# One matmul chain for B, C and dt of a selective scan, and the low parts of the B split moved by DMA

## The chip, the cores and the metric

One core of a Trainium2 chip runs the whole program. The metric is the device time of one execution in microseconds (us). Differences within about 0.2% are hard to tell from none for this kernel.

## What is computed

The network is two Mamba layers, a per-channel convolution stage and two attention and MLP layers over four images of 64 by 64 tokens with 96 channels. The change touches the Mamba layers alone. For each layer (channels DIN = 192, states 16, rank 6):

```python
dbl = xc @ xproj_w                      # 38 columns
dt, Bm, Cm = dbl[..., :6], dbl[..., 6:22], dbl[..., 22:]
delta = softplus(dt @ dt_w + dt_b)
dA  = exp(delta[..., None] * A)
dBx = delta[..., None] * Bm[:, :, None, :] * xc[..., None]
h   = scan(h[t] = dA[t] * h[t-1] + dBx[t])     # along the 4096 tokens
y   = (einsum('blds,bls->bld', h, Cm) + Dp * xc) * silu(z)
```

## The kernel before

**Tiles and steps.** `mamba_phase` works in 32 steps. A step is one layer, one pair of images and one chunk of 512 tokens (`ORDER`). The 2 x 192 channels of the pair lie in three groups of 128 partitions: image 0 channels 0 to 127, image 1 the same, and the last 64 channels of both. A step has 48 units, one for each group and state.

**One unit.** PE spreads the B row of the unit over 128 partitions of a PSUM bank (`broadcast_b`, four banks). DVE multiplies the bank by `dx` = delta * xc (`scale_unit`) and scans it with the decay from ACT (`scan_unit`). GpSimd (POOL) multiplies the states by the C row (`unit`), which one DMA has spread over 128 partitions (`load_c`, two states to a load, four loads ahead). PE adds the products up in PSUM (`add_up`).

**Slots.** Every engine has its program written out by hand as slots, one to a unit, and runs it in order. In slot t PE does `broadcast_b(t + 3)`, the epilogue of the step before, `add_up(t - 5)`, then a piece of the prologue of the next step. DVE does `scale_unit(t + 1)`, `scan_unit(t)`, then its extra operations. ACT does `unit(t + 4)` (the decay), a carry copy in every fourth slot, then its extras. A prologue matmul of PE in slot t stands ahead of `broadcast_b(t + 4)`, which DVE needs between its scans of units t + 2 and t + 3: there a long slot of PE shows. An extra of DVE in slot t lies between its scans of units t and t + 1. "Slot 34" below is always the slot in which DVE scans unit 34 of a step.

**The prologue.** Two tables, `EARLY` for the prologues of 30 steps (one of them runs before the first scan) and `LATE` for two, give the slots: layer norm, the projections to x and z (`x01`, `x2`, `z2`, `z01`), two SiLUs on ACT (`silu_x`, `silu_z`, each between two table loads), then the projection to B, C and dt (`proj`), and from dt the softplus chain (`dt`, `v`, `soft`).

**B in three bf16 parts.** B is split in high, middle and low bf16 parts, so that the spreading matmul can be bf16 with 96 rows (3 parts x 2 images x 16 states). `proj` computes B three times, on partitions 0 to 95 (with dt on 96 to 107) of bank 0: six fp32 matmuls, three of 108 columns into bank 0 and three of 32 columns (C) into bank 1. Then the split works in place:

```python
act.activation(dt_rows[rows, :], mm[rows, 0, :], ACT.Copy)          # "hi", L540
act.activation(b_rows[step % 2][:, :], mm[0:DT_AT, 0, :], ACT.Copy)  # "hi", L541, all 96 rows
dve: mm[0:64] -= b_rows[0:64]                                        # "rest", L636
act: b_rows[0:64] = mm[0:64]                                         # "mid",  L548
dve: b_rows[0:32] = mm[0:32] - b_rows[0:32]                          # "low",  L640
```

C is copied to `c32` (L545), stored to DRAM by SP (`store_c`, before the load with number 20 of 24 in a step) and read back spread. SP issues every DMA of this phase, in order.

Of the kernel before, what the change touches and what calls it, by code (L numbers as in the profile page):

```python
# [35 lines left out]
DT_AT = SPLITS * BC_ROWS  # L36
EPS = 1e-5
# [5 lines left out]
for c in range(CHUNKS):  # L43
# [13 lines left out]
    "proj": [30, 31, 32, 33, 34, 35], "hi": [35, 36], "rest": [37], "mid": [38], "low": [39],  # L57
    "dt": [37, 40, 41], "v": [38, 41, 42], "soft": [39, 40, 41, 42, 43, 44],
# [6 lines left out]
    "proj": [29, 29, 30, 30, 31, 31], "hi": [32, 32], "rest": [33], "mid": [34], "low": [35],  # L65
    "dt": [34, 36, 37], "v": [35, 37, 38], "soft": [37, 38, 39, 40, 41, 42],
# [5 lines left out]
SP_AT = 8  # L72
# [16 lines left out]
def bank_uses():  # L89

    table, count = {}, [0, 0]
    for w in range(-1, STEPS + 1):
        norm, rest = [MEAN, VAR], [X_FIRST, G2, Z_FIRST, PROJ, STEP, STEP2]
        out = [OUT] if w >= 1 else []
        if w + 1 >= STEPS:
            stages = out
        elif is_late(w + 1):
            stages = out + norm + rest
        else:
            stages = norm + out + rest  # L100
        for bank in range(2):
            for stage in stages:
                if stage != STEP2 or bank == 1:
                    table[bank, w, stage] = count[bank]
                    count[bank] += 1
    return table
# [23 lines left out]
def mamba_phase(nc, dram, f_dram, x_stats, f_stats):  # L130

    c_dram = nc.dram_tensor("c_map", (2, 2, STATES, CHUNK), FP32, kind="Internal").ap()


    with ExitStack() as ctx:
        def sb(name, shape, dtype=FP32):
# [8 lines left out]
        w_proj = sb("w_proj", [128, 2, GROUPS, DT_AT + 2 * RANK + BC_ROWS])  # L145
        w_dt = sb("w_dt", [DT_AT + 2 * RANK, 2, GROUPS, 128])
# [18 lines left out]
        tmp2 = sb("tmp2", [128, GROUPS, CHUNK])  # L165
# [5 lines left out]
        c32 = sb("c32", [BC_ROWS, CHUNK])  # L171
        dt_rows = sb("dt_rows", [DT_AT + 2 * RANK, CHUNK])
# [21 lines left out]
            (w_proj[:, :, :, :], dram["w_proj"][:, :, :, 0:DT_AT + 2 * RANK + BC_ROWS]),  # L194
            (w_dt[DT_AT:DT_AT + 2 * RANK, :, :, :], dram["w_dt"]),
# [4 lines left out]
        with nc.semaphore("a_exp") as a_exp, nc.semaphore("w_turned") as w_turned, \  # L200
                nc.semaphore("turned_copied") as turned_copied, nc.semaphore("w_folded") as w_folded:
            turned = dt_rows[0:C, 0:2 * 128].rearrange("p (k n) -> p k n", k=2)
# [42 lines left out]
        names = ["x0_loaded", "x1_loaded", "c0_loaded", "c1_loaded", "c2_loaded", "c3_loaded", "c_stored",  # L245
# [8 lines left out]
        (x0_loaded, x1_loaded, c0_loaded, c1_loaded, c2_loaded, c3_loaded, c_stored,  # L254
# [23 lines left out]
        with nc.Block() as block:  # L278
            @block.sync
            def _(sp):  # L280
                def load_x(pair, c):
                    sp.dma_start(x_in[pair][:, :, :],
                                 dram["x"][:, 2 * pair:2 * pair + 2, c * CHUNK:c * CHUNK + CHUNK]).then_inc(x_loaded[pair], 16)

                def load_c(i):

                    k, at = divmod(i, C_LOADS)
                    g, part = divmod(at, C_LOADS // GROUPS)
                    if at == 0:
                        sp.wait_ge(c_stored, 16 * (k + 1))  # L290
                    if i >= C_RING:
                        sp.wait_ge(multiplied, C_STATES * (i - C_RING + 1))
                    for r0, r1, b in (((0, 128, 0),), ((0, 128, 1),), ((0, HALF, 0), (HALF, 128, 1)))[g]:
                        rows = c_dram[k % 2, b, C_STATES * part:C_STATES * part + C_STATES, :].rearrange("s n -> (s n)")
                        sp.dma_start(c_rows[r0:r1, i % C_RING, :, :].rearrange("p s n -> p (s n)"),
                                     rows.unsqueeze(0).to_broadcast([r1 - r0, C_STATES * CHUNK])).then_inc(c_loaded[i % C_RING], 16)

                def store_c(step):

                    sp.wait_ge(bank1_read, USE[1, step - 1, PROJ] + 1)  # L300
                    sp.dma_start(c_dram[step % 2, :, :, :].rearrange("b s n -> (b s) n"), c32[:, :]).then_inc(c_stored, 16)

                def finish(w):

                    layer, pair, c = ORDER[w - 1]
                    for b in range(2):
                        sp.wait_ge(bank_read[b], USE[b, w, OUT] + 1)
                    if layer == 1:
                        sp.dma_start(f_dram[:, 2 * pair:2 * pair + 2, (c + 1) * CHUNK:(c + 2) * CHUNK],
                                     fused[pair][:, :, :]).then_inc(f_stored[pair], 16)  # L310
                    elif c + 1 < CHUNKS:
                        load_x(pair, c + 1)

                load_x(0, 0)
                load_x(1, 0)
                store_c(0)
                for i in range(C_RING):
                    load_c(i)
                for w in range(STEPS):
                    for at in range(C_LOADS):  # L320
                        i = C_LOADS * w + at + C_RING
                        if at == C_LOADS - C_RING and w + 1 < STEPS:
                            store_c(w + 1)
                        if i < STEPS * C_LOADS:
                            load_c(i)
                        if at == SP_AT and w >= 1:
                            finish(w)
                finish(STEPS)
                for pair in range(2):
                    sp.wait_ge(f_stored[pair], 16 * CHUNKS)  # L330

            @block.tensor
            def _(pe):
# [4 lines left out]
                def broadcast_b(n):  # L338
                    k, u = divmod(n, STEP_UNITS)
                    g, s = divmod(u, STATES)  # L340
                    if u == 0:
                        pe.wait_ge(bank0_read, USE[0, k - 1, PROJ] + 1)
# [31 lines left out]
                def prologue(w, at, step):  # L374
# [41 lines left out]
                    for i in due(plan["proj"], at):  # L416
                        g, bank = divmod(i, 2)
                        if g == 0:
                            fill(bank, w, PROJ)
                        pe.wait_ge(xc_ready, step + 1)  # L420
                        rows, off = ((DT_AT + 2 * RANK, 0), (BC_ROWS, DT_AT + 2 * RANK))[bank]
                        last = pe.matmul(mm[0:rows, bank, :], w_proj[:, layer, g, off:off + rows],  # L422
                                         xc[step % 2][:, g, :], start=g == 0, stop=g == GROUPS - 1)
                        if g == GROUPS - 1:
                            last.then_inc(bank_full[bank], 1)
                    for g in due(plan["dt"], at):
# [4 lines left out]
                        rows = slice(DT_AT, DT_AT + 2 * RANK)  # L431
# [15 lines left out]
            def _(act):  # L447
# [27 lines left out]
                def softplus(step, g, stage):  # L475
# [5 lines left out]
                    if stage == 1:  # L481
# [5 lines left out]
                        act.activation(tmp2[:, g, :], zpre[:, g, :], ACT.Ln).then_inc(log_ready, 1)  # L487
                        act.activation(zpre[:, g, :], zpre[:, g, :], ACT.Copy, bias=-1.0).then_inc(um_ready, 1)

                def prologue(w, at, step):  # L490
# [45 lines left out]
                    for i in due(plan["hi"], at):  # L536
                        act.wait_ge(bank_full[i], USE[i, w, PROJ] + 1)
                        if i == 0:
                            rows = slice(DT_AT, DT_AT + 2 * RANK)
                            act.activation(dt_rows[rows, :], mm[rows, 0, :], ACT.Copy).then_inc(dt_copied, 1)  # L540
                            act.activation(b_rows[step % 2][:, :], mm[0:DT_AT, 0, :], ACT.Copy).then_inc(hi_ready, 1)  # L541
                        else:
                            if step > 0:
                                act.wait_ge(c_stored, 16 * step)
                            act.activation(c32[:, :], mm[0:BC_ROWS, 1, :], ACT.Copy).then_inc(bank_read[1], 1)  # L545
                    for i in due(plan["mid"], at):
                        act.wait_ge(rest_ready, step + 1)
                        act.activation(b_rows[step % 2][0:2 * BC_ROWS, :], mm[0:2 * BC_ROWS, 0, :],  # L548
                                       ACT.Copy).then_inc(mid_ready, 1)
# [26 lines left out]
            def _(dve):  # L576
# [49 lines left out]
                def prologue(w, at, step):  # L626
# [6 lines left out]
                    for i in due(plan["rest"], at):  # L633
                        dve.wait_ge(dt_copied, step + 1)
                        dve.wait_ge(hi_ready, step + 1)
                        dve.tensor_tensor(mm[0:2 * BC_ROWS, 0, :], mm[0:2 * BC_ROWS, 0, :],  # L636
                                          b_rows[step % 2][0:2 * BC_ROWS, :], ALU.subtract).then_inc(rest_ready, 1)
                    for i in due(plan["low"], at):
                        dve.wait_ge(mid_ready, step + 1)
                        dve.tensor_tensor(b_rows[step % 2][0:BC_ROWS, :], mm[0:BC_ROWS, 0, :],  # L640
                                          b_rows[step % 2][0:BC_ROWS, :], ALU.subtract).then_inc(bank_read[0], 1)
# [16 lines left out]
            def _(pool):  # L658
# [8 lines left out]
                def softplus(step, g, stage):  # L667
# [6 lines left out]
                    if stage == 3:  # L674
                        pool.wait_ge(lost_ready, nth)
                        pool.tensor_tensor(tmp2[:, g, :], tmp2[:, g, :], tmp1[:, g, :], ALU.subtract).then_inc(log1p_ready, 1)
                    if stage == 4:
                        pool.wait_ge(log1p_ready, nth)
                        pool.tensor_tensor(delta[into][:, g, :], xpre[:, g, :], tmp2[:, g, :], ALU.add).then_inc(delta_ready, 1)
# [869 lines left out]
```

## Time and profile before

| | |
|---|---|
| median of three runs | 4724.49 us (4716.68 to 4725.94) |
| the profiled execution, its own time | 4725.55 us |
| its span | 4723.4 us |
| first scan to last scan (Mamba phase) | 83.31 to about 3132.6 us |
| busy PE, DVE, ACT, POOL over the span | 4159.9, 3580.9, 2405.8, 2469.5 us |

Matmuls are pipelined, so a busy PE is not a PE at its limit. The starts of the scans are the clock of this kernel: a step is the time from one scan of unit 0 to the next.

### The profile page before, as it was taken

The numbers are of one execution on the slowest core, as the hardware profiler recorded it, in microseconds if no ns is written. First come the engines' busy times: TensorE is split into PE (matmuls) and PEld (weight loads), VectorE is DVE, ScalarE is ACT, GpSimd is POOL, SyncE is SP. The second block draws the span as 40 slices with busy tenths as digits, with TensorE's granted clock in tenths as the row PEclk, the third lists the DMA queues.
The fourth block names the chain that finished last, engine by engine and source line by source line (L and its number), as shares of the span: only waits on it lengthen the run. The fifth ranks groups of instructions, "written<-read, shape, count | busy, mean of one in ns | idle before, by whom it ended". The sixth has DMA issues, their size and how long they took to land. (4 is left out here: it accounts for less than half of the span.)

```text
span 4723.4 us, 44868 instructions
## 1 busy us (share of the span) xinstructions
PE 4159.9 (88%) x13922; PEld 1790.8 (38%) x13922; DVE 3580.9 (76%) x4409; ACT 2405.8 (51%) x3937; POOL 2469.5 (52%) x1988
## 2 busy tenths in 40 slices
PE   6999999999999999999999999841989889888964
PEld 2333333333333333333333333311546546555543
DVE  3999999999999999999999999974115415414345
ACT  4666666666666666666766676621013222312223
POOL 3778887888778877887788778740000000000000
PEclk8999999999999999999999999985999999999976
DMA  3444444444444444444444444433010020000000
GB/s 91 141 130 137 136 143 134 135 137 145 135 133 138 142 137 137 136 138 141 136 138 133 144 132 138 126 88 88 21 38 21 6 53 17 17 15 4 17 0 14
DMA packets 135882, 462.03 MB, mean 98 GB/s; under 512 B 20783, under 2 KB 23282, under 8 KB 133822
## 3 DMA queue, kind: packets, MB, share of 16 engines
q1 hardware_dynamic: 135646, 459.18, 32.6%
q8 instruction: 112, 1.84, 0.2%
q14 instruction: 124, 1.02, 0.1%
HBM read 433.64 MB, written 20.97 MB: 96 GB/s over the span
## 5 line engine op out<-in xcount | busy, mean ns | idle before, releaser
L664 POOL TENSOR_TENSOR prod<-states,c_rows 128x512 f32<-128x512 f32 x1536 | 1939.6, 1279 | 589.2 <-DVE states L596 573.6
L596 DVE TENSOR_TENSOR_SCAN states<-decay,carry,bpsum 128x512 f32<-128x512 f32 x1536 | 1937.8, 1262 | 0.0
L353 PE MATMUL ypsum<-prod,identity 128*128 128x512 f32 x3072 | 1582.4, 596 | 0.4 <-POOL prod L664 0.3
L455 ACT ACTIVATE decay<-delta,decay_rate 128x512 f32<-128x512 f32 x1536 | 1078.4, 716 | 722.1 <-DVE states L596 623.4
L583 DVE TENSOR_TENSOR bpsum<-bpsum,dx 128x512 f32<-128x512 f32 x1536 | 1034.9, 674 | 89.8 <-PE bpsum L346 71.7
L346 PE MATMUL bpsum<-b_rows,select 96*128 96x512 bf16 x1536 | 594.2, 387 | 167.6 <-DVE states L596 166.0
L353 PEld LDWEIGHTS ypsum<-prod,identity 128*128 128x128 f32 x3072 | 590.2, 194 | 309.4 <-issue 175.3
L346 PEld LDWEIGHTS bpsum<-b_rows,select 96*128 96x128 bf16 x1536 | 147.7, 96 | 1072.8 <-DVE states L596 669.4
L1063 PE MATMUL convp<-img_hi,w_hi 96*96 96x512 f16 (+1 forms) x1568 | 485.3, 387 | 59.0 <-PEq L1441 43.1
L1411 DVE SCALAR_TENSOR_TENSOR x<-convp,unscale,x_group 96x1024 f32<-96x1024 f32 x16 | 20.4, 1278 | 407.9 <-PE convp L1063 407.9
L1063 PE MATMUL convp<-img_hi,w_lo 128*96 128x512 f16 (+1 forms) x896 | 276.0, 387 | 0.0
L1063 PE MATMUL convp<-img_lo,w_hi 96*96 96x512 f16 x896 | 274.8, 384 | 0.0
L1063 PEld LDWEIGHTS convp<-img_hi,w_hi 96*96 96x96 f16 (+1 forms) x1568 | 193.0, 124 | 200.1 <-issue 64.7
L401 PE MATMUL mm<-h_norm,w_xs 96*64 96x512 f32 x512 | 267.5, 616 | 0.0
L393 PE MATMUL mm<-h_norm,w_xs 96*128 96x512 f32 x512 | 262.9, 599 | 2.7 <-ACT h_norm L509 2.7
L1221 ACT ACTIVATE t_next<-convp 128x768 f32<-128x768 f32 x16 | 12.9, 808 | 438.3 <-PE convp L1074 438.3
L1063 PE MATMUL convp<-img_lo,w_mid 128*96 128x512 f16 x672 | 207.9, 386 | 0.0
L422 PE MATMUL mm<-xc,w_proj 128*32 128x512 f32 (+1 forms) x384 | 199.6, 604 | 0.0
L1083 PE MATMUL tp<-ident,haug 128*96 128x128 f32 (+1 forms) x512 | 84.9, 295 | 99.3 <-DVE haug L1328 98.8
L519 ACT ACTIVATE xpre<-mm,cols 128x512 f32<-128x512 f32 x96 | 65.7, 685 | 200.5 <-PE mm L401 106.2
L1198 ACT ACTIVATE haug<-dev_t 128x3072 f32<-128x3072 f32 x16 | 44.2, 2765 | 207.2 <-DVE dev_t L1321 207.2
L393 PEld LDWEIGHTS mm<-h_norm,w_xs 96*128 96x128 f32 x512 | 98.0, 192 | 128.6 <-issue 123.8
(215 smaller groups left out, 4531.6 us busy)
## 6 DMA issues: line engine op xcount, KB each, us to landing
c_rows<-c_map SPq DMA_DIRECT2D x512, 512.0 KB, 3.7
c_rows<-c_map SPq DMA_DIRECT2D x512, 256.0 KB, 3.9
x_in<-in_x SPq DMA_DIRECT2D x16, 384.0 KB, 6.0
fused_map<-fused SPq DMA_DIRECT2D x16, 384.0 KB, 5.1
work<-fused_map SPq DMA_DIRECT2D x4, 1536.0 KB, 9.6
x<-in_x SPq DMA_DIRECT2D x4, 1536.0 KB, 15.8
x_biased_map<-work SPq DMA_DIRECT2D x4, 1536.0 KB, 7.1
x_group<-x_biased_map SPq DMA_DIRECT2D x16, 384.0 KB, 3.7
```

Of the source, the lines that this page charges most:

```text
L346: pe.matmul(bpsum[:, n % B_BANKS, :], pick, b_rows[k % 2][:, :], start=True, stop=True).then_inc(b_full, 1)
L353: pe.matmul(ypsum[:, group % Y_BANKS, :], identity[:, :], prod[:, n % P_RING, :], start=s == 0, stop=s == STATES - 1).then_inc(summed, 1)
L393: last = pe.matmul(mm[:, b, :], w_xs[:, layer, k, 0:128], h_norm[:, b, k:k + CHUNK], start=k == 0, stop=k == TAPS - 1)
L401: last = pe.matmul(mm[b * HALF:b * HALF + HALF, 0, :], w_xs[:, layer, k, 128:DIN], h_norm[:, b, k:k + CHUNK], start=k == 0, stop=k == TAPS ...
L422: last = pe.matmul(mm[0:rows, bank, :], w_proj[:, layer, g, off:off + rows], xc[step % 2][:, g, :], start=g == 0, stop=g == GROUPS - 1)
L455: act.activation(decay[:, n % RING, :], delta[k % 2][:, g, :], ACT.Exp, scale=decay_rate[:, ORDER[k][0], g, s:s + 1]).then_inc(decay_ready, 1)
L519: act.activation(xpre[:, g, :], mm[:, g % 2, :], ACT.Identity, bias=cols[:, layer, g, at_conv:at_conv + 1]).then_inc(bank_read[g % 2], 1)
L583: dve.tensor_tensor(bpsum[:, n % B_BANKS, :], bpsum[:, n % B_BANKS, :], dx[k % 2][:, g, :], ALU.mult).then_inc(scaled, 1)
L596: dve.tensor_tensor_scan(states[:, n % H_RING, :], decay[:, n % RING, :], bpsum[:, n % B_BANKS, :], carry[:, at, u:u + 1], ALU.mult, ALU.a ...
L664: pool.tensor_tensor(prod[:, n % P_RING, :], states[:, n % H_RING, :], c_rows[:, n // C_STATES % C_RING, n % C_STATES, :], ALU.mult).then_ ...
L1063: last = pe.matmul(convp[0:C, g % 2, half, :], w, img[0:rows, r:r + GROUP_ROWS // 2, kx:kx + SIDE], start=product == 0, stop=i >= CONV_MMS ...
L1083: last = pe.transpose(tp[0:rows, fill % 2, j * TILE:(j + 1) * TILE], haug[:, 4 * c + j, 0:rows], ident[:, :])
```

## The change

B is projected once. The 76 columns (B 32, C 32, dt 12) are one chain of three fp32 matmuls into bank 0. ACT copies dt, then B and C together in fp32 (`bc32`, 64 rows), then the high part of B, all three in one slot. The middle and the low part are computed on partitions 0 to 31 and moved by two small DMAs of SP to partitions 32 to 63 and 64 to 95 of `b_rows` (`move_b`). B and C rows are stored together (`store_rows`), the loads read C from that store. The first `broadcast_b` of a step waits for both moves. The slots of `proj` and of all that follows it are moved: in `EARLY` `hi` from 35 and 36 to 33, `rest` from 37 to 34, `mid` from 38 to 35, `low` from 39 to 36, the dt matmuls and the softplus three slots or so forward. `tmp2` shrinks to one group, with a wait for the group before.

```diff
+C_FROM, DT_ROW = DT_AT + 2 * RANK, 2 * BC_ROWS
...
-    "proj": [30, 31, 32, 33, 34, 35], "hi": [35, 36], "rest": [37], "mid": [38], "low": [39],
-    "dt": [37, 40, 41], "v": [38, 41, 42], "soft": [39, 40, 41, 42, 43, 44],
+    "proj": [30, 31, 32], "hi": [33], "rest": [34], "mid": [35], "low": [36],
+    "dt": [34, 37, 36], "v": [35, 38, 37], "soft": [36, 37, 38, 39, 40, 41],
...
-    "proj": [29, 29, 30, 30, 31, 31], "hi": [32, 32], "rest": [33], "mid": [34], "low": [35],
-    "dt": [34, 36, 37], "v": [35, 37, 38], "soft": [37, 38, 39, 40, 41, 42],
+    "proj": [29, 30, 31], "hi": [32], "rest": [33], "mid": [34], "low": [35],
+    "dt": [33, 36, 35], "v": [34, 37, 36], "soft": [35, 36, 37, 38, 39, 40],
...
-SP_AT = 8
+SP_AT, SP_ROWS_AT, SP_MOVE_AT = 8, 16, 17
...
-                if stage != STEP2 or bank == 1:
+                if bank == (1 if stage == STEP2 else 0 if stage == PROJ else bank):
...
-        tmp2 = sb("tmp2", [128, GROUPS, CHUNK])
+        tmp2 = sb("tmp2", [128, CHUNK])
...
-        c32 = sb("c32", [BC_ROWS, CHUNK])
-        dt_rows = sb("dt_rows", [DT_AT + 2 * RANK, CHUNK])
+        b_mid = sb("b_mid", [BC_ROWS, CHUNK], BF16)
+        b_low = sb("b_low", [BC_ROWS, CHUNK], BF16)
+        bc32 = sb("bc32", [2 * BC_ROWS, CHUNK])
+        dt_rows = sb("dt_rows", [DT_ROW + 2 * RANK, CHUNK])
...
-            (w_proj[:, :, :, :], dram["w_proj"][:, :, :, 0:DT_AT + 2 * RANK + BC_ROWS]),
-            (w_dt[DT_AT:DT_AT + 2 * RANK, :, :, :], dram["w_dt"]),
+            (w_proj[:, :, :, 0:BC_ROWS], dram["w_proj"][:, :, :, 0:BC_ROWS]),
+            (w_proj[:, :, :, BC_ROWS:DT_ROW], dram["w_proj"][:, :, :, C_FROM:C_FROM + BC_ROWS]),
+            (w_proj[:, :, :, DT_ROW:], dram["w_proj"][:, :, :, DT_AT:DT_AT + 2 * RANK]),
+            (w_dt[DT_ROW:DT_ROW + 2 * RANK, :, :, :], dram["w_dt"]),
...
-            turned = dt_rows[0:C, 0:2 * 128].rearrange("p (k n) -> p k n", k=2)
+            turned = decay[0:C, 0, 0:2 * 128].rearrange("p (k n) -> p k n", k=2)
...
+                def broadcast_rows(kind, k, g, first, count, tile, loaded):
+                    for r0, r1, b in (((0, 128, 0),), ((0, 128, 1),), ((0, HALF, 0), (HALF, 128, 1)))[g]:
+                        rows = bc_dram[k % 2, kind, b, first:first + count, :].rearrange("s n -> (s n)")
+                        sp.dma_start(tile[r0:r1], rows.unsqueeze(0).to_broadcast([r1 - r0, count * CHUNK])).then_inc(loaded, 16)
                 def load_c(i):
                     k, at = divmod(i, C_LOADS)
                     g, part = divmod(at, C_LOADS // GROUPS)
                     if at == 0:
-                        sp.wait_ge(c_stored, 16 * (k + 1))
+                        sp.wait_ge(rows_stored, 16 * (k + 1))
                     if i >= C_RING:
                         sp.wait_ge(multiplied, C_STATES * (i - C_RING + 1))
-                    for r0, r1, b in (((0, 128, 0),), ((0, 128, 1),), ((0, HALF, 0), (HALF, 128, 1)))[g]:
-                        rows = c_dram[k % 2, b, C_STATES * part:C_STATES * part + C_STATES, :].rearrange("s n -> (s n)")
-                        sp.dma_start(c_rows[r0:r1, i % C_RING, :, :].rearrange("p s n -> p (s n)"),
-                                     rows.unsqueeze(0).to_broadcast([r1 - r0, C_STATES * CHUNK])).then_inc(c_loaded[i % C_RING], 16)
-
-                def store_c(step):
-
-                    sp.wait_ge(bank1_read, USE[1, step - 1, PROJ] + 1)
-                    sp.dma_start(c_dram[step % 2, :, :, :].rearrange("b s n -> (b s) n"), c32[:, :]).then_inc(c_stored, 16)
+                    broadcast_rows(1, k, g, C_STATES * part, C_STATES,
+                                   c_rows[:, i % C_RING, :, :].rearrange("p s n -> p (s n)"), c_loaded[i % C_RING])
+                def store_rows(step):
+                    sp.wait_ge(rows_ready, step + 1)
+                    sp.dma_start(bc_dram[step % 2, :, :, :, :].rearrange("k b s n -> (k b s) n"), bc32[:, :]).then_inc(rows_stored, 16)
+                def move_b(step):
+                    sp.wait_ge(mid_ready, step + 1)
+                    sp.dma_start(b_rows[step % 2][BC_ROWS:2 * BC_ROWS, :], b_mid[:, :]).then_inc(b_moved, 16)
+                    sp.wait_ge(bank0_read, USE[0, step - 1, PROJ] + 1)
+                    sp.dma_start(b_rows[step % 2][2 * BC_ROWS:, :], b_low[:, :]).then_inc(b_moved, 16)
...
-                store_c(0)
+                store_rows(0)
+                move_b(0)
                 for i in range(C_RING):
                     load_c(i)
                 for w in range(STEPS):
                     for at in range(C_LOADS):
                         i = C_LOADS * w + at + C_RING
-                        if at == C_LOADS - C_RING and w + 1 < STEPS:
-                            store_c(w + 1)
+                        if at == SP_ROWS_AT and w + 1 < STEPS:
+                            store_rows(w + 1)
+                        if at == SP_MOVE_AT and w + 1 < STEPS:
+                            move_b(w + 1)
...
-                        pe.wait_ge(bank0_read, USE[0, k - 1, PROJ] + 1)
+                        pe.wait_ge(hi_ready, k + 1)
+                        pe.wait_ge(b_moved, 32 * (k + 1))
...
-                    for i in due(plan["proj"], at):
-                        g, bank = divmod(i, 2)
+                    for g in due(plan["proj"], at):
                         if g == 0:
-                            fill(bank, w, PROJ)
-                        pe.wait_ge(xc_ready, step + 1)
-                        rows, off = ((DT_AT + 2 * RANK, 0), (BC_ROWS, DT_AT + 2 * RANK))[bank]
-                        last = pe.matmul(mm[0:rows, bank, :], w_proj[:, layer, g, off:off + rows],
+                            fill(0, w, PROJ)
+                            pe.wait_ge(xc_ready, step + 1)
+                        last = pe.matmul(mm[0:DT_ROW + 2 * RANK, 0, :], w_proj[:, layer, g, :],
                                          xc[step % 2][:, g, :], start=g == 0, stop=g == GROUPS - 1)
                         if g == GROUPS - 1:
-                            last.then_inc(bank_full[bank], 1)
+                            last.then_inc(bank0_full, 1)
...
-                        rows = slice(DT_AT, DT_AT + 2 * RANK)
+                        rows = slice(DT_ROW, DT_ROW + 2 * RANK)
...
-                        act.activation(tmp2[:, g, :], zpre[:, g, :], ACT.Ln).then_inc(log_ready, 1)
+                        if nth > 1:
+                            act.wait_ge(delta_ready, nth - 1)
+                        act.activation(tmp2[:, :], zpre[:, g, :], ACT.Ln).then_inc(log_ready, 1)
...
                     for i in due(plan["hi"], at):
-                        act.wait_ge(bank_full[i], USE[i, w, PROJ] + 1)
-                        if i == 0:
-                            rows = slice(DT_AT, DT_AT + 2 * RANK)
-                            act.activation(dt_rows[rows, :], mm[rows, 0, :], ACT.Copy).then_inc(dt_copied, 1)
-                            act.activation(b_rows[step % 2][:, :], mm[0:DT_AT, 0, :], ACT.Copy).then_inc(hi_ready, 1)
-                        else:
-                            if step > 0:
-                                act.wait_ge(c_stored, 16 * step)
-                            act.activation(c32[:, :], mm[0:BC_ROWS, 1, :], ACT.Copy).then_inc(bank_read[1], 1)
+                        act.wait_ge(bank0_full, USE[0, w, PROJ] + 1)
+                        rows = slice(DT_ROW, DT_ROW + 2 * RANK)
+                        act.activation(dt_rows[rows, :], mm[rows, 0, :], ACT.Copy).then_inc(dt_copied, 1)
+                        if step > 0:
+                            act.wait_ge(rows_stored, 16 * step)
+                        act.activation(bc32[:, :], mm[0:2 * BC_ROWS, 0, :], ACT.Copy).then_inc(rows_ready, 1)
+                        act.activation(b_rows[step % 2][0:BC_ROWS, :], mm[0:BC_ROWS, 0, :], ACT.Copy).then_inc(hi_ready, 1)
                     for i in due(plan["mid"], at):
                         act.wait_ge(rest_ready, step + 1)
-                        act.activation(b_rows[step % 2][0:2 * BC_ROWS, :], mm[0:2 * BC_ROWS, 0, :],
-                                       ACT.Copy).then_inc(mid_ready, 1)
+                        if step > 0:
+                            act.wait_ge(b_moved, 32 * step)
+                        act.activation(b_mid[:, :], mm[0:BC_ROWS, 0, :], ACT.Copy).then_inc(mid_ready, 1)
...
-                        dve.wait_ge(dt_copied, step + 1)
                         dve.wait_ge(hi_ready, step + 1)
-                        dve.tensor_tensor(mm[0:2 * BC_ROWS, 0, :], mm[0:2 * BC_ROWS, 0, :],
-                                          b_rows[step % 2][0:2 * BC_ROWS, :], ALU.subtract).then_inc(rest_ready, 1)
+                        dve.tensor_tensor(mm[0:BC_ROWS, 0, :], mm[0:BC_ROWS, 0, :],
+                                          b_rows[step % 2][0:BC_ROWS, :], ALU.subtract).then_inc(rest_ready, 1)
                     for i in due(plan["low"], at):
                         dve.wait_ge(mid_ready, step + 1)
-                        dve.tensor_tensor(b_rows[step % 2][0:BC_ROWS, :], mm[0:BC_ROWS, 0, :],
-                                          b_rows[step % 2][0:BC_ROWS, :], ALU.subtract).then_inc(bank_read[0], 1)
+                        if step > 0:
+                            dve.wait_ge(b_moved, 32 * step)
+                        dve.tensor_tensor(b_low[:, :], mm[0:BC_ROWS, 0, :], b_mid[:, :], ALU.subtract).then_inc(bank_read[0], 1)
```

## Rows read from the trace of the kernel before

**Rows 1.** The waits of DVE, 200 to 3000 us: total, times, longest.

```profile
DVE bpsum L583 <- PE bpsum L346: 65.3, 191, 2.0
```

**Rows 2.** Busy time by engine: one stretch, and the whole step of four stretches.

```profile
1098.14:1119.90 21.76, 21.76 (x55) 7.71 (x53) 20.90 (x25) 18.37 (x32) 13.29 (x11) 1.00 0.47 121
...
sum 94.87, PE 90.13 PEld 31.22 DVE 93.35 ACT 63.30 POOL 77.17; mean PE 22.53 PEld 7.81 DVE 23.34 ACT 15.83 POOL 19.29
```

**Rows 3.** Timeline of PE: start us, duration, line, shapes, count.

```profile
1100.99 0.38 PE L346 MATMUL bpsum<-b_rows,select 96*128 96x512 bf16 x1
...
1102.07 1.02 PE L422 MATMUL mm<-xc,w_proj 128*108 128x512 f32 x2
1102.93 0.38 PE L346 MATMUL bpsum<-b_rows,select 96*128 96x512 bf16 x1
...
1104.10 1.05 PE L422 MATMUL mm<-xc,w_proj 128*32 128x512 f32 x2
1105.08 0.39 PE L346 MATMUL bpsum<-b_rows,select 96*128 96x512 bf16 x1
```

**Rows 4.** Timeline of DVE in the same step.

```profile
1102.02 1.27 DVE L596 TENSOR_TENSOR_SCAN states<-decay,carry,bpsum 128x512 f32<-128x512 f32 x1
...
1112.14 1.27 DVE L596 TENSOR_TENSOR_SCAN states<-decay,carry,bpsum 128x512 f32<-128x512 f32 x1
1113.33 0.67 DVE L636 TENSOR_TENSOR mm<-mm,b_rows 64x512 f32<-64x512 f32 x1
...
1114.51 1.26 DVE L596 TENSOR_TENSOR_SCAN states<-decay,carry,bpsum 128x512 f32<-128x512 f32 x1
...
1116.94 1.26 DVE L596 TENSOR_TENSOR_SCAN states<-decay,carry,bpsum 128x512 f32<-128x512 f32 x1
...
1118.71 0.67 DVE L640 TENSOR_TENSOR b_rows<-mm,b_rows 32x512 bf16<-32x512 f32 x1
...
1119.90 1.26 DVE L596 TENSOR_TENSOR_SCAN states<-decay,carry,bpsum 128x512 f32<-128x512 f32 x1
...
1121.67 1.26 DVE L596 TENSOR_TENSOR_SCAN states<-decay,carry,bpsum 128x512 f32<-128x512 f32 x1
```

**Rows 5.** Timeline of ACT in the same step.

```profile
1106.52 0.72 ACT L455 ACTIVATE decay<-delta,decay_rate 128x512 f32<-128x512 f32 x1
...
1107.24 1.93 ACT L455 ACTIVATE decay<-delta,decay_rate 128x512 f32<-128x512 f32 x3
1111.32 0.59 ACT L540 ACTIVATE dt_rows<-mm 12x512 f32<-12x512 f32 x1 [2.14 <-PE mm L422]
1111.93 0.59 ACT L541 ACTIVATE b_rows<-mm 96x512 bf16<-96x512 f32 x1
1112.43 0.71 ACT L455 ACTIVATE decay<-delta,decay_rate 128x512 f32<-128x512 f32 x1
```

**Rows 6.** Timeline of ACT where the late plan runs.

```profile
3014.91 0.19 ACT L463 ACTIVATE carry<-states 128x4 f32<-128x4 f32 x1
3015.86 0.59 ACT L540 ACTIVATE dt_rows<-mm 12x512 f32<-12x512 f32 x1 [0.75 <-PE mm L422]
3016.47 0.59 ACT L541 ACTIVATE b_rows<-mm 96x512 bf16<-96x512 f32 x1
```

**Rows 7.** Timeline of DVE at that place.

```profile
3017.17 0.69 DVE L636 TENSOR_TENSOR mm<-mm,b_rows 64x512 f32<-64x512 f32 x1 [1.15 <-ACT b_rows L541]
```

**Rows 8.** DMA issues: count, KB each, us to landing.

```profile
c_rows<-c_map SPq DMA_DIRECT2D x512, 512.0 KB, 3.7
...
c_map<-c SPq DMA_DIRECT2D x32, 64.0 KB, 3.8
```

**Rows 9.** Timeline of ACT in the opening, before the first scan.

```profile
66.82 1.28 ACT L535 ACT_TABLE_LOAD   x1
70.06 0.59 ACT L540 ACTIVATE dt_rows<-mm 12x512 f32<-12x512 f32 x1 [1.96 <-PE mm L422]
...
73.01 0.69 ACT L554 ACTIVATE tmp<-mm,cols 128x512 f32<-128x512 f32 x1 [0.32 <-PE mm L432]
```

More of the change, by code:

```diff
@@ L130, in mamba_phase @@
 def mamba_phase(nc, dram, f_dram, x_stats, f_stats):
-    c_dram = nc.dram_tensor("c_map", (2, 2, STATES, CHUNK), FP32, kind="Internal").ap()
+    bc_dram = nc.dram_tensor("bc_map", (2, 2, 2, STATES, CHUNK), FP32, kind="Internal").ap()
     with ExitStack() as ctx:
@@ L144, in mamba_phase @@
         w_z = sb("w_z", [C, 2, DIN])
-        w_proj = sb("w_proj", [128, 2, GROUPS, DT_AT + 2 * RANK + BC_ROWS])
-        w_dt = sb("w_dt", [DT_AT + 2 * RANK, 2, GROUPS, 128])
+        w_proj = sb("w_proj", [128, 2, GROUPS, DT_ROW + 2 * RANK])
+        w_dt = sb("w_dt", [DT_ROW + 2 * RANK, 2, GROUPS, 128])
         w_out = sb("w_out", [128, 2, 2, C])
@@ L243, in mamba_phase @@
             nc.all_engine_barrier(sem_only=True)
-        names = ["x0_loaded", "x1_loaded", "c0_loaded", "c1_loaded", "c2_loaded", "c3_loaded", "c_stored",
+        names = ["x0_loaded", "x1_loaded", "c0_loaded", "c1_loaded", "c2_loaded", "c3_loaded", "rows_ready", "rows_stored", "b_moved",
                  "b_full", "decay_ready", "scaled", "scanned",
@@ L253, in mamba_phase @@
         sems = [ctx.enter_context(nc.semaphore(n)) for n in names]
-        (x0_loaded, x1_loaded, c0_loaded, c1_loaded, c2_loaded, c3_loaded, c_stored,
+        (x0_loaded, x1_loaded, c0_loaded, c1_loaded, c2_loaded, c3_loaded, rows_ready, rows_stored, b_moved,
          b_full, decay_ready, scaled, scanned, carry_saved, multiplied,
@@ L675, in softplus @@
                         pool.wait_ge(lost_ready, nth)
-                        pool.tensor_tensor(tmp2[:, g, :], tmp2[:, g, :], tmp1[:, g, :], ALU.subtract).then_inc(log1p_ready, 1)
+                        pool.tensor_tensor(tmp2[:, :], tmp2[:, :], tmp1[:, g, :], ALU.subtract).then_inc(log1p_ready, 1)
                     if stage == 4:
                         pool.wait_ge(log1p_ready, nth)
-                        pool.tensor_tensor(delta[into][:, g, :], xpre[:, g, :], tmp2[:, g, :], ALU.add).then_inc(delta_ready, 1)
+                        pool.tensor_tensor(delta[into][:, g, :], xpre[:, g, :], tmp2[:, :], ALU.add).then_inc(delta_ready, 1)
                     if stage == 5:
```

## The prediction

> **What bounds the kernel now.** I read the waits of DVE first. In 2800 us of the Mamba phase DVE waits 65.3 us for the spreading matmul of B [rows 1] and for next to nothing else. So the step is DVE's own work plus a little of PE. The busy times of one whole step say the same: DVE 93.35 and PE 90.13 of 94.87 us, ACT 63.30 and POOL 77.17 [rows 2]. ACT has a third of its time free, as a mean. The question is what it has at the place that the change moves to.
>
> Then I read the starts of the scans. With nothing extra a unit takes DVE 1.77 us (1121.67 - 1119.90) [rows 4]. A unit with one small DVE operation behind its scan takes 2.37 (1114.51 - 1112.14, with "rest"), one with the skip 2.43 (1116.94 - 1114.51). The unit with gate and low takes 2.96, so with the gate alone some 2.37 (a small operation adds 0.60). These are the DVE-bound slots. In the others of this stretch PE sets the pace. A PE slot with a 108-column projection takes 1.94 us from one spreading matmul to the next, one with the 32-column projection 2.15 [rows 3], both over 1.77.
>
> The stretch to compare is from the scan of unit 32 (1102.02) to that of unit 40 (1119.90): 17.88 us [rows 4]. Ahead of it nothing is moved, and behind it units take 1.77. It is that of the 29 prologues of the early plan that run under scans (the 30th is the opening); I worked it out for this step and take it for all.
>
> **The change: what it gives PE.** Three of the six projection matmuls go. They were in slots 31, 33 and 35. The gaps that the scans then have, by slot: 32 and 33 each 1.94 (PE's slots 30 and 31), 34 with "rest" 2.37, 35 1.77, 36 with "low" 2.37, 37 1.77, 38 with the skip 2.43, 39 with the gate alone 2.37. Sum 16.96, against 17.88: 0.92 us less a step, if nothing new is waited for. A 76-column matmul has no row here. Its PE slot is bounded by 1.94 and 2.15; I take 1.94, as 76 is nearer to 108 than to 32. It will turn out not to matter.
>
> DVE's work is not less: "rest" has 32 rows for 64, and the "low" operation on 32 rows and the "rest" on 64 both take 0.67 [rows 4].
>
> **What it asks of ACT.** This is the step that decides. "rest" moves from slot 37 to 34, and needs the high part of B, which ACT copies in slot 33. Follow ACT in its own order [rows 5]. The SiLU of z with its two table loads fills slot 31, and ACT comes out of it at 1106.52, with the decay of slot 32. The carry copy follows, and at 1107.24 three decays at once, of slots 33, 34 and 35, which ACT was behind with: 0.61 us each (1.93 for three, the last 0.72). In the kernel before ACT then waits 2.14 us for PE, so it is early for `hi`. After the change `hi` stands behind the decay of slot 33 alone:
>
> - the decay of slot 33 at 1107.24, so the dt copy at 1107.85 (PE is done by then: slot 31 at 1102.93, slot 32 at 1104.87, its matmul 1.08 later, 1.02 long: 1106.97; with 2.15 for the slots, 1107.4)
> - the copy of B and C 0.61 later, at 1108.46 (the pace from the dt copy to the next is 0.61 [rows 5])
> - the high part 0.50 later, at 1108.96 (from L541 to the next is 0.50 [rows 5]; the new copies have 64 and 32 rows, but all these copies run along 512 elements, and 12 rows and 96 rows both took 0.59)
> - "rest" 0.70 behind the start of that copy, at 1109.66 (3016.47 to 3017.17 where DVE did wait for it [rows 6, 7]).
>
> DVE is there sooner: scan 33 at 1103.96, scan 34 at 1105.90, "rest" free to start 1.19 later (1112.14 to 1113.33 [rows 4]), at 1107.09. It stands 2.57 us. DVE runs in order, so behind it stand the scale of unit 35 and the scan after it, and for these wait POOL, PE and ACT. PE's gain is inside this wait, and so is the doubt about 76 columns.
>
> From "rest" to the next scan is 1.18 (1113.33 to 1114.51), so scan 35 starts at 1110.84. Then 1.77, 2.37, 1.77, 2.43, 2.37: scan 40 at 1121.55, where it was 1119.90. A step of the early plan gets 1.65 us longer: -0.92 + 2.57. Times 29: **+47.8 us**.
>
> The old order shows the same wait where the late plan has "rest" one slot behind `hi`: DVE stood 1.15 us by the profile's account [rows 7]. There ACT waited 0.75 us for PE [rows 6]; now it goes on at once: dt 0.1 behind the start of the carry copy (3014.91), "rest" 0.61 + 0.50 + 0.70 later, at 3016.82 for 3017.17. Two steps: **-0.7 us** (none to -1.5).
>
> **The opening.** Before the first scan nothing runs beside the chain. ACT waits 1.96 us for the six matmuls [rows 9]. With three, the dt copy starts when the table load is done, at 68.10 for 70.06. The extra copy ahead of the high part gives back 0.5, but the old dt matmul waited for C's copy. I take **-1.8 us** (bounds -1.4 and -1.96). The loads of `w_proj` come as three DMAs of small pieces for one: no row shows that; between -1 (fewer bytes) and +3, taken as 0.
>
> **The moves and the stores, costed at nothing.** `low` starts at about 1113.8 and is done by 1114.5. A transfer from issue to landing takes 3.7 or 3.8 us [rows 8]; the moves are of 32 KB, for 64 KB of the old store. So b_moved is there by 1119. The first spreading matmul of the next step stands in PE's slot 45, behind the scan of unit 44, which ends near 1121.6 + 4 x 1.77 + 1.3 = 1129.9: cover 10 us. If that were gone, each us late is a us a step. SP holds two loads of C while it waits: number 16 until the store is issued (about 1109.1), number 17 until `low` is done (1114.5). They land by 1113.5 and 1119.5, for units 40 and 42, which POOL takes up after 1122.8 and 1126.4: cover 7 us or more. The wait for `tmp2` is on a delta some 20 slots old. `mid` on ACT waits for "rest" (done 1110.4), and the first dt matmul needs only the dt copy, as PE is ahead again. "low" is 2 slots behind "rest", and ACT has the middle part by 1111.4.
>
> **Sum.** 47.8 - 0.7 - 1.8 = +45.3. On the profiled execution's own 4725.55: 4770.9. The median of the runs is 1.06 lower, so 4769.8; I say **4770 us**, 1.0% slower. Bounds: the stall can be 0.4 shorter (dt copy to the next at 0.50, a quicker handover) or 0.5 longer a step, so +34 to +61; with the opening, 4755 to 4789.
>
> **One rule against a row.** The paces of ACT's copies are 0.61 and 0.50 [rows 5]. The Trainium skill, ScalarE: Activation LUTs, Rules for kernel authors, budgets 0.3 us an ACTIVATE and 0.83 ns an element, so an estimate of 0.72 us for 512 elements. By it the stall would be longer, and the whole about 4783; the trace does not agree for the copies that it shows.
>
> **Rivals.**
> 1. *ACT is in time, and PE's gain stands (faster).* For it: ACT idles a third of a step, and waits for PE at this very place before the change. Against it: it is now asked for two decays sooner and has one copy more to make first. It decides at one point: "rest" must start before 1108.01 (1119.90 less the 11.89 from "rest" to scan 40), so the high part before 1107.31, when ACT is still on the decay of slot 33. If there is no stall: 29 x -0.92 = -26.7, the late plans three matmuls of 1.02 us each, so up to -6.1 for both (an estimate: their PE slots hold two of them), -1.8: 4690.9, **4690 us**. 10%.
> 2. *A second wait as well (slower yet).* SP is the suspect: two waits in its queue in front of the loads, and two moves. For it: every DMA of the phase goes by this queue. Against it: covers of 7 and 10 us. If the landing took 1 us more than a cover, +31: **4801 us**. 8%.
> 3. *ACT's copies of 64 rows are longer than those seen*, by some 0.16 each: 29 x 0.47 = +13.6: **4783 us**. 6%. This is what the skill's budget would make of it.
> 4. *ACT comes out of the SiLU earlier once PE is lighter*, so that stall and gain cancel: **4725 us**. 4%. Against it: the table load starts behind z's copies, which the change leaves alone.
>
> Forecast: 72%. Faster by over 0.2% is rival 1 and a quarter of rival 4: 0.11. Within 0.2% (what measurement can tell): 0.03. Slower: 0.86. The range of 8 in 10 is 4742 to 4800; the forecast's own is 4755 to 4789.
>
> **What would show it.** Right: DVE's "rest" waits for ACT's copy of the high part about 2.6 us in each step, some 75 us over the phase; the waits of DVE for the spreading matmul fall; the step shown here 96.5 us long. ACT no longer waits for the projection. Wrong: no wait at "rest", and that step near 94 us; or the wait is at the spreading matmul of unit 0 or in POOL for a load of C.

## The result, and the profile after

| | us |
|---|---|
| before, median of the runs | 4723.89 |
| after, median of 4 runs | 4778.0 (4775.46 to 4779.35) |
| ratio | 1.0117, 95% interval 1.0099 to 1.0134 |
| forecast | 4770 (range 4742 to 4800) |
| profiled execution after, its span | 4777.2 |

The waits of DVE in the same 2800 us, after (total us, times, longest):

```profile
DVE mm L654 <- ACT b_rows L563: 73.5, 29, 3.0
DVE bpsum L602 <- PE bpsum L366: 46.0, 138, 2.0
```

The first row is new. It is 29 waits at "rest" for ACT's copy of the high part: 28 steps of the early plan with 2.52 us each by the profile's account, and one of the two late steps with 2.98 (the first early step and the second late one lie outside these 2800 us, and have the same waits). The wait for the spreading matmul is down from 65.3 [rows 1] to 46.0: the gain is there, and it is small. Here is the stretch from the scan of unit 32 to that of unit 40, on DVE:

```profile
1023.03 1.27 DVE L615 TENSOR_TENSOR_SCAN states<-decay,carry,bpsum 128x512 f32<-128x512 f32 x1
...
1026.90 1.27 DVE L615 TENSOR_TENSOR_SCAN states<-decay,carry,bpsum 128x512 f32<-128x512 f32 x1
1030.69 0.69 DVE L654 TENSOR_TENSOR mm<-mm,b_rows 32x512 f32<-32x512 f32 x1 [2.52 <-ACT b_rows L563]
...
1031.90 1.26 DVE L615 TENSOR_TENSOR_SCAN states<-decay,carry,bpsum 128x512 f32<-128x512 f32 x1
...
1033.67 1.26 DVE L615 TENSOR_TENSOR_SCAN states<-decay,carry,bpsum 128x512 f32<-128x512 f32 x1
1034.85 0.65 DVE L660 TENSOR_TENSOR b_low<-mm,b_mid 32x512 bf16<-32x512 f32 x1
...
1036.03 1.26 DVE L615 TENSOR_TENSOR_SCAN states<-decay,carry,bpsum 128x512 f32<-128x512 f32 x1
...
1042.60 1.26 DVE L615 TENSOR_TENSOR_SCAN states<-decay,carry,bpsum 128x512 f32<-128x512 f32 x1
```

It takes 19.57 us (1042.60 - 1023.03) for 17.88 before [rows 4]; the forecast was 19.53. DVE was free for "rest" at 1028.09 (1026.90 and the 1.19 of [rows 4]) and started it at 1030.69: it stood 2.60 us, for 2.57 forecast. Everything around it goes at the paces forecast: 1.77 and 2.36 behind it. ACT at the same place:

```profile
1027.53 0.72 ACT L473 ACTIVATE decay<-delta,decay_rate 128x512 f32<-128x512 f32 x1
...
1028.26 0.70 ACT L473 ACTIVATE decay<-delta,decay_rate 128x512 f32<-128x512 f32 x1
1028.98 0.59 ACT L559 ACTIVATE dt_rows<-mm 12x512 f32<-12x512 f32 x1
1029.60 0.59 ACT L562 ACTIVATE bc<-mm 64x512 f32<-64x512 f32 x1
1030.09 0.57 ACT L563 ACTIVATE b_rows<-mm 32x512 bf16<-32x512 f32 x1
```

The decay of slot 33 starts at 1028.26, then the dt copy, the copy of B and C and the high part start 0.72, 0.62 and 0.49 us apart, and "rest" 0.60 behind the last. A step like that of [rows 2] went from 94.87 to 96.56 us (+1.69; forecast +1.65). Three early steps are longer still, that of [rows 2] among them; they come under the clock of PE below.

The moves and the store, from issue to landing (count, KB each, us):

```profile
bc_map<-bc SPq DMA_DIRECT2D x32, 128.0 KB, 2.3
...
b_rows<-b_mid SPq DMA_DIRECT2D x32, 32.0 KB, 3.3
b_rows<-b_low SPq DMA_DIRECT2D x32, 32.0 KB, 1.8
```

`low` is done by 1035.5; its move lands some 2 us after its issue, and the first spreading matmul that needs it comes after the scan of unit 44, at about 1051. The cover of 10 us stands. In these 2800 us POOL waits for DVE, PE and ACT, and not once for a load of C.

### The profile page after: what moved, and what is told of

Read it like the earlier page. It is cut to its first block and busy times, and to the rows that moved or that the text cites. A ratio compares the mean times of both kernels' runs of the same rounds, so it can differ in the third digit from the quotient of the medians.

```text
span 4777.2 us, 44613 instructions
## 1 busy us (share of the span) xinstructions
PE 4114.0 (86%) x13730; PEld 1784.4 (37%) x13730; DVE 3575.6 (75%) x4409; ACT 2420.3 (51%) x3937; POOL 2470.5 (52%) x1988
## 3 DMA queue, kind: packets, MB, share of 16 engines
q14 instruction: 126, 1.02, 0.1%
## 5 line engine op out<-in xcount | busy, mean ns | idle before, releaser
L373 PE MATMUL ypsum<-prod,identity 128*128 128x512 f32 x3072 | 1609.7, 606 | 0.4 <-POOL prod L683 0.3
L373 PEld LDWEIGHTS ypsum<-prod,identity 128*128 128x128 f32 x3072 | 599.8, 197 | 305.1 <-issue 170.8
L1102 PE MATMUL tp<-ident,haug 128*96 128x128 f32 (+1 forms) x512 | 84.9, 296 | 99.3 <-DVE haug L1347 98.8
L692 POOL TENSOR_TENSOR tmp<-zpre,tmp 128x512 f32<-128x512 f32 x96 | 122.0, 1270 | 42.5 <-ACT zpre L508 42.5
```

The source lines that it names most:

```text
L373: pe.matmul(ypsum[:, group % Y_BANKS, :], identity[:, :], prod[:, n % P_RING, :], start=s == 0, stop=s == STATES - 1).then_inc(summed, 1)
L692: pool.tensor_tensor(tmp1[:, g, :], zpre[:, g, :], tmp1[:, g, :], ALU.subtract).then_inc(lost_ready, 1)
L1102: last = pe.transpose(tp[0:rows, fill % 2, j * TILE:(j + 1) * TILE], haug[:, 4 * c + j, 0:rows], ident[:, :])
```

## The experiments

All are built from the changed kernel unless it is said otherwise. Times are medians, beside the kernel before on the same chip (4723.19 us for the first four, 4724.76 for the last four).

**rest36: the split two slots later.**

```diff
-"hi": [33], "rest": [34], "mid": [35], "low": [36], "dt": [34, 37, 36], "v": [35, 38, 37],
+"hi": [33], "rest": [36], "mid": [37], "low": [38], "dt": [34, 39, 36], "v": [35, 40, 37],
-SP_MOVE_AT = 17
+SP_MOVE_AT = 18
```

> The changed kernel, with only the split of B two slots later in the early plan (rest 36, mid 37, low 38, the second dt matmul behind it at 39). Theory (DVE stands for ACT's copy of the high part, which is ready 3.76 us after DVE starts the scan of unit 34): DVE reaches rest at 4.73 us after that start, so there is no wait. The stretch from the scan of unit 32 to that of unit 40 is 16.96 us, for 19.6 in the changed kernel and 17.88 in the one before. 29 x 2.57 = 74.5 us less than the changed kernel's 4778: about 4702, faster than before by 0.5%. Rival (the moves, the stores or PE's waits cost the time): still near 4778, with a wait at the spreading matmul of unit 0 or in POOL. Rival (the projection never was a price): 4725.

Measured: 4701.69 us, ratio 0.9954 (0.9937 to 0.9971). DVE in the stretch:

```profile
1004.79 1.27 DVE L615 TENSOR_TENSOR_SCAN states<-decay,carry,bpsum 128x512 f32<-128x512 f32 x1
...
1006.73 1.27 DVE L615 TENSOR_TENSOR_SCAN states<-decay,carry,bpsum 128x512 f32<-128x512 f32 x1
...
1008.50 1.27 DVE L615 TENSOR_TENSOR_SCAN states<-decay,carry,bpsum 128x512 f32<-128x512 f32 x1
1009.69 0.66 DVE L654 TENSOR_TENSOR mm<-mm,b_rows 32x512 f32<-32x512 f32 x1
```

"rest" starts 1.19 us after its scan: no wait. The same matmuls, copies and DMAs, waiting for the same things, are now faster than the kernel before. The stretch takes 17.11 us (1000.92 to 1018.03), where I had said 16.96. With "rest" gone from slot 34, that slot shows PE's 1.94 (1004.79 to 1006.73), which it had hidden.

**rest35: one slot later.** The same edit with 35, 36, 37 and dt at 38.

> The same with the split one slot later (rest 35, mid 36, low 37). Theory: DVE reaches rest 2.96 us after the start of the scan of unit 34 and stands 0.80 us a step; 29 x 1.77 = 51.3 us less than the changed kernel: 4727, the same as before. Rivals: 4778 as for the other.

Measured: 4722.4 us, ratio 1.0 (0.9991 to 1.001). "rest" starts 1.85 us after its scan, for the 1.19 without a wait: it stands 0.66 us in each early step (0.58 by the profile's account), for 0.80 expected. DVE comes to it 0.17 later than expected, as PE's 1.94 in slot 34 comes to light here too; the stretch takes 17.80 us, 1.77 less than in the changed kernel, as expected. Three places of the split give 4778, 4722 and 4702: each slot is worth what DVE does in it, until the wait is used up.

**dt_last: the copies in another order.** The edit in words:

```diff
-act: dt copy, copy of B and C, high part
+act: copy of B and C, high part, dt copy
```

> The changed kernel with ACT's three copies in the order B and C, high part of B, dt. Theory (the price is the queue in front of the high part on ACT, priced by copies): rest starts 0.61 us sooner in every step, the dt matmul 1.1 us later with room. 31 x 0.61 = 18.9 us less: 4759. Rival (DVE waits for something else that ends at the same time): 4778.

Measured: 4751.83 us, ratio 1.0065 (1.0048 to 1.0081). 26 us less, for 19. ACT there:

```profile
1020.04 0.70 ACT L473 ACTIVATE decay<-delta,decay_rate 128x512 f32<-128x512 f32 x1
1020.65 0.57 ACT L561 ACTIVATE bc<-mm 64x512 f32<-64x512 f32 x1
1021.13 0.57 ACT L562 ACTIVATE b_rows<-mm 32x512 bf16<-32x512 f32 x1
```

The first copy of 64 rows starts 0.61 us after the decay (1020.04 to 1020.65), where the dt copy of 12 rows started 0.72 after it, and the next follows in 0.48, where behind the dt copy it took 0.62. So the dt copy held "rest" up by 0.75 us a step (4.25 us for 5.00 from the scan of unit 34 to the next), and 31 x 0.75 is 23. In the profiled executions 24.6 us of the difference lie between the first scan and the last: those 23, and 1.4 because three steps of the changed kernel are 2.8 longer than their like (the clock of PE, below), and here one late and one early step are 1.4 longer together. The order of three small copies is worth nearly half of the loss.

**no_moves: B without its middle and low part.** The two DMAs of `move_b` are left out, the waits for them become waits for `low`, and the rows of `b_rows` for the two parts are zero.

> The changed kernel without the two moves of B: the middle and the low part stay where they are computed, and the rows of b_rows for them are zero, so B counts with its high part alone. The first spreading matmul waits for low directly. Theory (the moves are covered by 10 us): 4778, within 3 us. Rival (SP's queue or the transfers take time from the step): up to 31 us less, near 4747.

Measured: 4778.28 us, ratio 1.012 (1.0103 to 1.0136), the same as the change. The moves have no part in the time. The store of B and C is still there in this run; but POOL waits for no load of C in either kernel, so the rest of rival 2 is out as well.

**silu_z34: the SiLU of z behind the high part on ACT.**

```diff
-"silu_z": [31]
+"silu_z": [34]
```

> The changed kernel with the SiLU of z, and its two table loads, in ACT's slot 34 in place of 31: behind the high part, in front of the middle part. Theory (ACT's order is the price): ACT comes to the high part as soon as PE has the projection, the wait at rest falls from 2.6 to about 1.7 us, and a new wait of about 1.7 us stands at low for the middle part; together 0.8 us a step more: about 4802. Rival (DVE's wait at rest is PE's lateness, not ACT's): the wait at rest stays 2.6.

Measured: 4832.97 us, ratio 1.0233 (1.0217 to 1.0249), 31 us more than expected. ACT and DVE in one step, then PE:

```profile
1045.34 0.59 ACT L559 ACTIVATE dt_rows<-mm 12x512 f32<-12x512 f32 x1 [2.96 <-PE mm L440]
...
1047.05 0.69 DVE L654 TENSOR_TENSOR mm<-mm,b_rows 32x512 f32<-32x512 f32 x1 [1.55 <-ACT b_rows L563]
...
1052.97 0.68 DVE L660 TENSOR_TENSOR b_low<-mm,b_mid 32x512 bf16<-32x512 f32 x1 [1.68 <-ACT b_mid L568]
...
1061.02 0.70 DVE L602 TENSOR_TENSOR bpsum<-bpsum,dx 128x512 f32<-128x512 f32 x1 [0.81 <-PE bpsum L366]
```

```profile
1049.80 1.02 PE L373 MATMUL ypsum<-prod,identity 128*128 128x512 f32 x2
1054.13 2.07 PE L450 MATMUL mm<-dt_rows,w_dt 12*128 12x512 f32 x2 [3.31 <-ACT xpre L574]
...
1056.53 1.92 PE L373 MATMUL ypsum<-prod,identity 128*128 128x512 f32 x2
```

The two waits are those expected, 1.55 and 1.68 us: with the SiLU out of the way ACT itself waits 2.96 us for PE's projection, so what is left of DVE's wait is no longer ACT's backlog, and the block of 4.1 us (two table loads and the SiLU) bites where it stands now. The rest of the loss is new. PE idles 3.31 us behind the stalled chain, and from then its matmuls take twice as long (two passes in 1.92 us for 1.02). So DVE waits again for the spreading matmul, 0.81 us, and the stretch takes 21.27 us. Early steps like this one are 2.07 us longer than in the changed kernel, for 0.8 expected.

**spread: the one chain in every second slot.**

```diff
-"proj": [30, 31, 32], "hi": [33], "rest": [34], "mid": [35], "low": [36],
-"dt": [34, 37, 36], "v": [35, 38, 37], "soft": [36, 37, 38, 39, 40, 41],
+"proj": [31, 33, 35], "hi": [36], "rest": [37], "mid": [38], "low": [39],
+"dt": [37, 40, 41], "v": [38, 41, 42], "soft": [39, 40, 41, 42, 43, 44],
-SP_ROWS_AT, SP_MOVE_AT = 16, 17
+SP_ROWS_AT, SP_MOVE_AT = 18, 19
```

> The one chain in every second slot (proj 31, 33, 35) and all behind it in the slots of the kernel before (hi 36, rest 37, mid 38, low 39, dt and softplus as before). Theory: PE catches up 0.69 us in each empty slot, so the scans of units 32 to 36 go at DVE's 1.77; the stretch from the scan of unit 32 to that of unit 40 is 5 x 1.77 + 2.37 + 2.43 + 2.97 = 16.6 us for 17.88 before, and there is no wait at rest. 29 x 1.26 = 36.5 less than before, and the opening some 1 us shorter: about 4686. Rival (the chain is worth only its three matmuls where they stand, 0.8 a step): 4700.

Measured: 4686.88 us, ratio 0.9921 (0.9908 to 0.9935). PE in one step:

```profile
1000.13 0.38 PE L366 MATMUL bpsum<-b_rows,select 96*128 96x512 bf16 x1
...
1001.21 1.02 PE L440 MATMUL mm<-xc,w_proj 128*76 128x512 f32 x2
1002.07 0.38 PE L366 MATMUL bpsum<-b_rows,select 96*128 96x512 bf16 x1
...
1003.15 0.38 PE L366 MATMUL bpsum<-b_rows,select 96*128 96x512 bf16 x1
```

A slot with a 76-column matmul takes PE 1.94 us (1000.13 to 1002.07), an empty one 1.08 (to 1003.15), and DVE's 1.77 is above their mean. The stretch takes 16.61 us, as expected. Beside rest36 this is another 15 us, got by placing the same three matmuls. Not all of it went as expected: in seven early steps the eight units behind the stretch take 14.62 us for 14.15, 3.3 us in all, with PE's clock at its lower level (below), and the part behind the last scan happened to be 2.7 us shorter than in the kernel before. The two nearly cancel, so that the match of 4687 with 4686 is partly luck.

**spread_all: with the late plan and the load as well.** In `LATE` "rest" goes from 33 to 35, mid to 36, low to 37, dt to 33, 38, 39; `w_proj` comes in its 76 columns and is loaded by one DMA.

> The same, with rest two slots later in the late plan too (35, mid 36, low 37), and w_proj laid out in its 76 columns so that one DMA loads it. Theory: the wait at rest in the two late steps (about 3 us each by the trace of the changed kernel) goes, and the load is 0.9 us shorter: 5 to 8 us under the run spread, about 4680. Rival (the late plan is bound by PE there): no less than 4684.

Measured: 4680.44 us, ratio 0.9906 (0.989 to 0.9921). A late step takes 98.10 us for 101.03, so both together 5.9. The loading ends at 20.05 us, where it ended at 22.6 in the changed kernel and 23.7 in spread, with three DMAs of small pieces, and at 21.7 before. The expectation gave the load 0.9; in these profiles it comes 2.5 to 3.7 us sooner.

**v_after_soft: the opening.**

```diff
-"v": [35, 38, 37]
+"v": [35, 39, 38]
```

> The changed kernel with the Abs and Relu of groups 1 and 2 one slot later (38, 39), behind the softplus of group 0. Theory (in the opening ACT stands with them in front of that softplus, for the third dt matmul): the first scan comes 2.7 us sooner, at 82.5 us, and the steps are as they were: 4775. Rival (the opening is longer by the load alone): first scan at 85.

Measured in one run: 4770.07 us, first scan at 81.1 us for 85.2. Of the 9.0 us between the two profiled executions, 4.1 are this and 4.7 lie behind the last scan, where the edit changes nothing; so the 2.7 is read from ACT's rows, and not from the whole time. ACT in the opening, after the change:

```profile
69.31 0.59 ACT L559 ACTIVATE dt_rows<-mm 12x512 f32<-12x512 f32 x1
...
73.37 0.61 ACT L498 ACTIVATE tmp<-tmp 128x512 f32<-128x512 f32 x1
75.62 0.69 ACT L573 ACTIVATE tmp<-mm,cols 128x512 f32<-128x512 f32 x1 [1.64 <-PE mm L450]
...
76.78 0.63 ACT L503 ACTIVATE zpre<-tmp 128x512 f32<-128x512 f32 x1
```

and in this kernel:

```profile
72.01 0.61 ACT L498 ACTIVATE tmp<-tmp 128x512 f32<-128x512 f32 x1
72.71 0.63 ACT L503 ACTIVATE zpre<-tmp 128x512 f32<-128x512 f32 x1
```

In the changed kernel ACT goes from the first softplus operation (73.37) to the Abs of another group, for which it waits 1.64 us on PE's matmul, and comes back to the softplus at 76.78. With the Abs moved it does so 0.70 us after the first one. From the dt copy to that operation are 7.47 us and 4.76: 2.7 us, as expected. The other 1.4 us of the first scan are earlier than the dt copy (67.95 for 69.31). The start of the program differs by as much between kernels that share it: the dt copy comes at 68.20 in no_moves, and the loading ends at 22.6 to 23.7 us in the eight kernels with the three small loads.

## Why the prediction came out as it did

**The stall and its price: right, by the mechanism named.** The wait is where it was put, on the pair named, in every step of the early plan, and of the size said: 2.60 us for 2.57. rest35 and rest36 take it away by the slot, and the time goes with it. dt_last moves it by the copies in front of it. The sum 29 x 1.65 = 47.8 is 29 x 1.69 = 49.0 in the trace. The whole came 8 us above the forecast, inside its range. Most of that is not the stall: 1.2 from the steps, 3.7 from the opening, 2.8 from the clock and 0.9 behind the last scan.

**The rivals.** Rival 1, that ACT is in time, is what rest36 makes of the kernel, and there the time is faster than before, though by 22 us and not 34: the early steps give 22.5 and not 26.7, the two late steps, where the wait stays, 0.7 and not 6.1, and the first scan comes 0.3 later than before and not 1.8 sooner. Rival 2 is out by no_moves and by POOL's waits. Rival 4 is out: the decay behind ACT's last table load starts 4.50 us after the scan of unit 32 in both kernels (1106.52 - 1102.02 [rows 4, 5] and 1027.53 - 1023.03), so ACT comes out of the SiLU no earlier.

**A pace off by 0.1.** I took 0.61 us from the decay to the dt copy, from decays that follow each other. It is 0.72, and the copy of B and C follows in 0.62. "rest" then follows the high part in 0.60 and not 0.70, so two errors cancel, and that the wait is right to 0.03 is luck. Rival 3 is out: the copies of 64 and 32 rows last 0.59 and 0.57 us, as those of 12 and 96 did. The budget of the Trainium skill (ScalarE: Activation LUTs, Rules for kernel authors) that the prediction put beside it is stated there for an ACTIVATE with a pointer as its bias. These copies are written without one, so the row did not bear on them.

**The PE gain: 0.92 a step, right only for this placement.** It holds where "rest" covers PE's slot. rest36 has 0.77, as the third slow slot comes to light.

**The late plan: right**, 101.01 us for 101.36 in each of its two steps, -0.7: ACT goes on at once, and "rest" is 0.35 us nearer to the start of its step. The wait there did not shrink, though. It grew from 1.15 [rows 7] to 2.98 us, as a lighter PE brings DVE to the place sooner; spread_all takes it away and gains 2.9 a step.

**The opening: wrong in sign.** I forecast -1.8 us; the first scan came 1.9 later (85.19 for 83.31). Two things were missed or taken as 0. The start with the three small loads of `w_proj` is 0.9 later (22.6 for 21.7), inside the bounds that I gave; over the eight kernels with these loads it is 0.8 to 2.0 later than in the one profile before, so this term is known only roughly. And I followed the chain to the softplus without reading the new table to its end. "v" of group 2 is now in slot 37, ahead of the softplus's second stage in the same slot. In the opening, where nothing paces the slots, ACT waits there for the third dt matmul. v_after_soft shows that this is 2.7 us. The dt copy itself was 1.95 nearer to the start of ACT's SiLU of x, as forecast.

**What was not foreseen: the clock of PE.** The granted clock in 200 to 3000 us has a mean of 1.00 before and 0.98 after. In three of the 29 early steps it cost time, like this (columns of the first view: window, PE, PEld, DVE, ACT, POOL busy, granted clock, DMA share, GB/s; the second is PE in the same step):

```profile
1126.00:1130.00 4.00, 3.15 (x8) 0.92 (x7) 2.76 (x4) 3.98 (x9) 0.28 (x2) 0.99 0.48 91
1130.00:1143.00 13.00, 13.00 (x18) 4.12 (x17) 12.38 (x15) 8.88 (x18) 9.62 (x8) 0.50 0.36 108
1143.00:1150.00 7.00, 6.77 (x18) 2.49 (x16) 6.92 (x8) 2.85 (x5) 7.00 (x7) 0.96 0.45 150
```

```profile
1125.67 1.02 PE L373 MATMUL ypsum<-prod,identity 128*128 128x512 f32 x2
...
1127.67 0.39 PE L366 MATMUL bpsum<-b_rows,select 96*128 96x512 bf16 x1
...
1129.77 0.52 PE L366 MATMUL bpsum<-b_rows,select 96*128 96x512 bf16 x1 [0.84 <-DVE states L615]
...
1134.32 1.91 PE L373 MATMUL ypsum<-prod,identity 128*128 128x512 f32 x2
1136.16 2.07 PE L450 MATMUL mm<-dt_rows,w_dt 12*128 12x512 f32 x2
```

In the window with the stall PE is busy 3.15 of 4 us: it idles 0.84 us, for a scan of the stalled DVE. Then the granted clock is 0.50, the lower of its two levels (1.2 GHz), for 13 us. The two passes that add a product up take 1.91 us for 1.02, a dt matmul 2.07 for 1.12, and DVE waits for the spreading matmul three times, 0.19 to 0.26 each, in slots where PE had been in time. Those three steps took 97.42, 97.55 and 97.51 us: 0.9, 1.0 and 0.9 over their like. So the span is +53.8: 49.0, -0.7, +1.9, +2.8 for the clock, and 0.9 behind the last scan (the sum is 53.9 by rounding). The last term I did not follow up; that part takes 1583.7 to 1590.6 us over the ten profiled executions, so 0.9 says nothing.

That the stall at "rest" makes the clock fall is not shown. Every early step of the changed kernel has the stall, and the clock falls in 15 stretches of 3.4 to 13.7 us in the Mamba phase, 92 us in all, of which three cost time. In rest36, where the early steps have no stall, there are eight stretches of 3.4 us that cost nothing. But spread has no stall in the early steps either, and its clock falls in 22 stretches, 163 us in all. Most of them come after PE idled 1.18 and 0.66 us while it waited for scans.

## What to carry to other kernels

An engine that is free a third of the time may be the last at the very place where a change asks it for something sooner: walk its queue in order, up to the instruction that the others wait for, before an operation is moved forward. Freed work on a second engine is best taken out where slots would otherwise stand close together, and the rest of the chain left where it was: the same chain gave +1.2% placed early and -0.8% placed late. Look at the granted clock of PE after any edit that opens gaps in its work: in silu_z34 and in spread it fell behind such gaps, and what had been hidden came to light.

## What the runs showed of the hardware

- In silu_z34 PE's clock was at its lower level for 10 us in each of the 29 early steps, from about the end of PE's 3.31 us without work, and its mean over 200 to 3000 us was 0.95. Steps there took 98.6 or 99.3 us, 1.3 more than the two waits account for; 1.1 of it is waiting for the spreading matmul.
- PE idled far less elsewhere when the clock fell: 0.84 us in the step of the changed kernel shown, 1.18 and then 0.66 in most of the falls of spread. The same gaps stand in other steps of both kernels without a fall at that place: what makes it fall in one step and not in the next stays open.
- A matmul of 76 columns goes at the pace of one of 108: 1.94 us for its slot in spread, where one of 32 columns took 2.15 [rows 3] and one of 64 columns 2.18 (in the changed kernel, 1002.82 to 1005.00). Fewer columns than 76 made the slot longer, and not shorter.
- A copy on ACT of 12 rows at partition 64 started 0.11 us later after a decay than one of 64 rows at partition 0 (0.72 in the changed kernel, 0.61 in dt_last), and the copy behind it another 0.14 (0.62 for 0.48). Rows and partitions changed together here, so which of them it is stays open.
- The small moves within SBUF, 32 KB, landed in 3.3 and 1.8 us, the store of 128 KB in 2.3.
